# Attention: roots over four slots, projection and v chunks in other pairs, expert weights in pieces of 1024

## The chip, the cores and the metric

One core of a Trainium2 chip runs the whole program in one launch. The metric is device time in microseconds. The kernel before takes 1556.12 us as the median of three runs (1555.55 to 1556.91).

## The reference

x has 16 sequences of 256 rows and 256 columns. A first block (norms, a folded gate, a merge with a style vector, a feed-forward part) makes x1. Then comes attention, and then eight experts that each take the 512 rows with the highest gate. The change touches the attention stage, so this is the part that matters:

```python
h = _ln(x, ln1_g, ln1_b) + shift
qkv = (h @ Wqkv.T).reshape(b, n, 3, H, HD)          # H = 16 heads, HD = 64
q = _ln(qkv[:, :, 0].transpose(0, 2, 1, 3), qn_g, qn_b)
k = _ln(qkv[:, :, 1].transpose(0, 2, 1, 3), kn_g, kn_b)
v = qkv[:, :, 2].transpose(0, 2, 1, 3)
scores = jnp.einsum('bhnd,bhmd->bhnm', q, k) / jnp.sqrt(jnp.float32(HD))
attn = jax.nn.softmax(scores, axis=-1)
o = jnp.einsum('bhnm,bhmd->bhnd', attn, v)
x = x + o.transpose(0, 2, 1, 3).reshape(b, n, H * HD) @ Wout.T
gate = jax.nn.softmax(tok @ Wgate.T, axis=-1)        # tok: all 4096 rows of x
# each expert: g = _ln of its rows; gelu(g @ fc1s + b1s) @ fc2s + b2s, times the gate, added to the rows
```

Every large product is made of three fp32r matmuls: both operands are split into a high and a low part (h, l), and the product low times low is left out. The experts' weights fc1s and fc2s are split the same way, during the attention stage, and stored in DRAM for the expert stage.

## The kernel before

The attention stage works on one sequence (batch) per step t, t = -2 to 16. The steps 2 to 11 are a hardware loop of five passes with two steps each; the others are written out. Step t has eight pairs s, one for each two heads of batch t. While batch t has its scores made, batch t-1 is projected, batch t+1 has its q and k normed and its v made, batch t+2 is layer-normed and its first chunks made, and x2 of batch t-2 is finished. A pair has two slots, 2s and 2s+1. All engines run the same steps in their own order, which is written out by hand; a queue is strictly in order and semaphores join them.

In a pair TensorE does, in this order: the scores of pair s (L1019), the transposes of the probabilities of the pair before (L1032), the fill of slot 2s, the chunks of this pair, a half of the projection if slot 2s holds it, the values matmuls (L1045) of the pair before, the fill of slot 2s+1. A chunk is 6 matmuls of 512 columns of the qkv product (L147, `product`); chunks 0 to 7 are q and k, 8 to 11 are v. A half of the projection is 24 matmuls of 256 columns. A fill is a group of transposes into the one bank `tr`: of h (`a` of the next batch), of q and k (eight, "qk" 0 to 7, L1102), of x2, or the gate products; ScalarE empties the bank (`empty`) before the next fill may use it (`tr_free`). TR_FILLS says which fill stands in which slot, CHUNK_PAIRS which pair a chunk is in.

VectorE does in a pair: `lowest_of` (L1346, the row minima of both heads' scores, whose q side carries a minus sign, which ScalarE's exponentials wait for), the low half of the output (L1365), the reciprocal of side 0 (L1352), the copy of `pT` for side 1 (L1377), and in between the pieces of its chains. `chains` has, in each slot, six spots. A root chain (`rsqrt_op`, L93 to L100, and L1294 ahead of it) is 12 small dependent operations on 128x32 for n=0 and 12 for n=1. SUM_SLOT is the slot in which it starts, and in the kernel before one operation stands in every spot. `total` (L1342) sums the squares of a chunk. At the end of odd pairs stands the subtraction that makes `ew_l` (L1406). In pair 5 stands a_h (L1400), which waits for `out_h` and for all twelve chunks of batch t+1.

ScalarE does the low-lag work: o_h, emptying `tr`, four exponentials (L1158), the copy of `pT` for side 0 (L1221), the outputs of the chunks, and at the end of even pairs `ew_h` (L1232). GpSimd does the norms of q and k (`norm`, L1244, in slots NORM_SLOT to NORM_SLOT+3; the first of each n waits for the roots), the two divisions of the probabilities by their sums (`divide`, L1249), in pair 5 between both divisions a_l (L1274, waits for a_h), in pair 6 rstd (L1264) and the sum for x2 (L1268). SP issues the loads and stores. For the experts' weights it moves four pieces of 512 columns in each step: load `ew_raw`, wait for `ew_l`, store both parts, load the next.

Of the kernel before, what the change touches and what calls it, by code (L numbers as in the profile page):

```python
# [15 lines left out]
F32 = mybir.dt.float32  # L16
# [3 lines left out]
ALU = mybir.AluOpType  # L20
# [186 lines left out]
def first_block(nc, a, exponent, banks, ident, x1_rows, hbias, cols, target_rows, load_attention, weights, rows_of, sbuf, sems):  # L207
# [4 lines left out]
    with s:  # L212
# [179 lines left out]
        with nc.Block() as block:  # L392
# [414 lines left out]
TR_FILLS = [("x2", 0, 1), ("gates", 0, 3), ("proj", 0, 4), ("qk", 0, 5), ("qk", 1, 6), ("qk", 2, 7), ("h", 0, 8), ("qk", 3, 9),  # L807
            ("proj", 1, 10), ("qk", 4, 11), ("qk", 5, 12), ("qk", 6, 13), ("qk", 7, 14)]
# [6 lines left out]
CHUNK_PAIRS = [6, 6, 7, 7, 0, 0, 1, 1, 3, 3, 4, 4]  # L815
AHEAD = 4

SUM_SLOT, NORM_SLOT = (2, 6), (4, 8)
SPOTS = 6
LN_SLOT, ROOT_PAIR, APPLY_SLOT = 10, 6, 13  # L820
SPLIT_PAIR = 5
OUT_STATS_PAIR, OUT_ROOT_PAIR, OUT_APPLY_PAIR = 7, 1, 2
X2_PAIR = 6
# [43 lines left out]
def attention(nc, exponent, weights, rows_of, banks, ident, x1_rows, hbias, cols, x2_rows, logit, out, a, halves, sbuf, sems):  # L867
# [4 lines left out]
    with s:  # L872
# [21 lines left out]
        ew_raw = sbuf(s, "ew_raw", [P, 512])  # L894
        ew_h, ew_l = (sbuf(s, f"ew_{p}", [P, 512], F32R) for p in "hl")
# [61 lines left out]
        with nc.Block() as block:  # L957
            @block.sync
            def _(sp):
                def load_piece(b, c):  # L960
                    if c < 2:
                        src = a["fc1s"][bass.ds(b * P, P), c * 512:(c + 1) * 512]
                        dst = ew_raw[:, :]
                    else:
                        src = a["fc2s"][bass.ds(b * (4 * P) + (c - 2) * 2 * P, 2 * P), :].rearrange("(k p) n -> p k n", p=P)
                        dst = ew_raw[:, :].rearrange("p (k n) -> p k n", n=D)
                    sp.dma_start(dst, src).then_inc(ew_in, 16)

                def pieces(b, cs):
                    for c in cs:  # L970
                        if live(b):
                            wait(sp, ew_lo, 4, b, c + 1)
                            for n, part in enumerate((ew_h, ew_l)):
                                sp.dma_start(halves[c // 2 * 2 + n][bass.ds(b, 1), :, c % 2 * 512:(c % 2 + 1) * 512].rearrange("s p n -> p (s n)"),
                                             part[:, :].bitcast(F32)).then_inc(ew_stored, 16)
                        nb, nc_ = (b, c + 1) if c < 3 else (b + 1, 0)
                        if live(b) and live(nb):
                            load_piece(nb, nc_)
# [3 lines left out]
                def step(t, odd):  # L982
                    pieces(t, (0,))
# [10 lines left out]
                    pieces(t, (1,))  # L994
# [4 lines left out]
                    pieces(t, (2,))  # L999
# [4 lines left out]
                    pieces(t, (3,))  # L1004
# [3 lines left out]
                sp.wait_ge(ew_stored, 128 * NB)  # L1008
# [142 lines left out]
            def _(act):  # L1151
# [54 lines left out]
                def step(t, odd):  # L1206
                    for s in range(PAIRS):
# [21 lines left out]
                        if live(t) and s % 2 == 0:  # L1229
                            wait(act, ew_in, 64, t, 16 * (s // 2 + 1))  # L1230
                            wait(act, ew_stored, 128, t, 32 * (s // 2))
                            nc.scalar.activation(ew_h[:, :], ew_raw[:, :], ACT.Copy).then_inc(ew_hi, 1)  # L1232
# [48 lines left out]
            def _(dve):  # L1281
                link = Links(dve, links)

                def chains(t, i, spot):
# [3 lines left out]
                    for n in range(TT):  # L1288

                        k = (i - SUM_SLOT[n]) * SPOTS + spot  # L1290
                        if live(new) and 0 <= k <= RSQRT_OPS:
# [62 lines left out]
                def step(t, odd):  # L1354
                    far = t + 2
                    for s in range(PAIRS):
# [46 lines left out]
                        if live(t) and s % 2 == 1:  # L1403
                            wait(dve, ew_hi, 4, t, s // 2 + 1)
                            wait(dve, ew_stored, 128, t, 32 * (s // 2))
                            nc.vector.tensor_tensor(ew_l[:, :], ew_raw[:, :], ew_h[:, :].bitcast(F32), ALU.subtract).then_inc(ew_lo, 1)  # L1406
# [481 lines left out]
```

## Time and profile before

| | us |
|---|---|
| median of three runs | 1556.12 |
| the profiled execution, its own time | 1554.05 |
| its span, first to last instruction | 1551.9 |
| TensorE busy | 1380.8 (89%) |
| VectorE busy | 1019.5 (66%) |
| ScalarE busy | 959.8 (62%) |
| GpSimd busy | 783.3 (50%) |

The attention stage with scores runs from 398.7 us to about 1256 us of the span; in its middle TensorE is busy for 294.9 of 300 us. The granted clock of TensorE there is 1.00 of 2.4 GHz. In the timelines a row is one instruction, or several of the same kind in a row: start, length, engine, line, operation, tiles, shape and count; in brackets stands the idle time of the engine before it and what ended it. PE is TensorE, DVE VectorE, ACT ScalarE, POOL GpSimd. Matmuls overlap, so what counts is from start to start. Lines L93 to L147 are helpers.

### The profile page before, as it was taken

Reading aid. Unit: us, or ns where it says so; the run is one execution under the profiler, and the core shown is the slowest. Engines: PE = TensorE matmul, PEld = TensorE weight load, DVE = VectorE, ACT = ScalarE, POOL = GpSimd, SP = SyncE. Lnnn points to the kernel's source line nnn. Section 1 sums busy time; section 2 is a strip of 40 time slices with the busy share of each in tenths; the row PEclk is TensorE's granted clock in tenths of the full one; section 3 lists DMA queues with packets and bytes.
Section 4 is the critical chain, followed back from the end, with each engine's and each line's share of the span. In section 5 each row is a group of like instructions: output and inputs, shape, how many; then the busy total and the mean of one; then the engine's idle time right before and its main releaser. Section 6 shows DMA issues by size and latency. Waiting matters only on the chain. (4 is left out here: it accounts for less than half of the span.)

```text
span 1551.9 us, 31212 instructions
## 1 busy us (share of the span) xinstructions
PE 1380.8 (89%) x9672; PEld 1132.0 (73%) x9672; DVE 1019.5 (66%) x2495; ACT 959.8 (62%) x2535; POOL 783.3 (50%) x736
## 2 busy tenths in 40 slices
PE   1599999997899999999999999999999852599996
PEld 1599999996567777777777776777777642498996
DVE  2686666744566777776777777677767566565642
ACT  2266656564677777778777877877787620335452
POOL 1377666654346555645654654565455410254633
PEclk9799999999999999999999999999999975699998
DMA  7122222110022222212222221222222253167652
GB/s 233 44 64 63 68 74 61 50 47 28 21 69 82 82 82 77 82 61 76 88 82 71 86 82 62 75 88 82 76 75 82 83 184 128 39 205 234 203 161 27
DMA packets 92407, 138.89 MB, mean 89 GB/s; under 512 B 8656, under 2 KB 61824, under 8 KB 92160
## 3 DMA queue, kind: packets, MB, share of 16 engines
q1 hardware_dynamic: 83600, 126.02, 24.3%
q0 software_dynamic: 6144, 8.39, 2.9%
q10 hardware_dynamic: 2544, 3.16, 0.6%
q8 instruction: 42, 0.69, 0.2%
q14 instruction: 77, 0.63, 0.1%
HBM read 87.20 MB, written 50.35 MB: 89 GB/s over the span
## 5 line engine op out<-in xcount | busy, mean ns | idle before, releaser
L1249 POOL TENSOR_TENSOR prob<-prob,share_p 128x512 f32<-128x512 f32 x256 | 268.1, 1053 | 329.5 <-DVE share_p L1352 329.5
L1158 ACT ACTIVATE prob<-bank,shift 128x256 f32<-128x256 f32 x512 | 236.1, 474 | 110.0 <-DVE shift L1346 109.8
L1346 DVE TENSOR_REDUCE shift<-bank 128x2 f32<-128x512 f32 x256 | 164.7, 685 | 194.8 <-PE bank L1019 189.8
L1244 POOL TENSOR_TENSOR raw_qk<-raw_qk,rq 128x512 f32<-128x512 f32 x128 | 145.6, 1149 | 65.3 <-DVE rq L100 65.3
L147 PE MATMUL bank<-wqkv_h,rowsT_h 128*128 128x512 f32 x384 | 160.7, 418 | 4.4 <-PEq L392 3.5
L1045 PE MATMUL bank<-pT,v 128*64 128x256 f32 x1024 | 139.6, 394 | 25.3 <-ACT pT L1221 25.3
L147 PE MATMUL bank<-wqkv_h,rowsT_l 128*128 128x512 f32 x384 | 152.2, 396 | 0.0
L147 PE MATMUL bank<-wqkv_l,rowsT_h 128*128 128x512 f32 x384 | 151.7, 395 | 0.0
L1019 PE MATMUL bank<-landing 64*128 64x256 f32 x1024 | 146.3, 404 | 3.1 <-ACT prob L1158 3.1
L1032 PEld LDWEIGHTS bank<-ident,prob 128*128 128x128 f32 x1024 | 109.8, 141 | 44.5 <-issue 42.1
L1032 PE MATMUL bank<-ident,prob 128*128 128x128 f32 x1024 | 141.2, 280 | 0.6 <-POOL prob L1249 0.4
L1045 PEld LDWEIGHTS bank<-pT,v 128*64 128x64 f32 x1024 | 62.4, 136 | 82.3 <-issue 31.4
L1019 PEld LDWEIGHTS bank<-landing 64*128 64x128 f32 x1024 | 88.7, 187 | 34.4 <-issue 23.0
L1177 ACT ACTIVATE landing<-bank,cols 128x512 f32<-128x512 f32 x128 | 102.3, 799 | 11.6 <-PE bank L1102 11.6
L1158 ACT ACTIVATION_READ_ACCUMULATOR prob<-bank,shift 128x1 f32 x512 | 104.3, 204 | 0.0
L630 POOL TENSOR_TENSOR hid_l<-hid,hid_h 128x512 fp32r<-128x512 f32 x64 | 85.9, 1351 | 32.7 <-ACT hid_h L547 31.9
L1199 ACT ACTIVATE raw_sq<-bank 128x512 f32<-128x512 f32 x128 | 79.4, 620 | 30.2 <-DVE ssq L1342 30.2
L543 ACT ACTIVATE hid<-bank,cols 128x256 f32<-128x256 f32 x128 | 53.4, 471 | 69.6 <-PE bank L147 69.6
L1342 DVE TENSOR_REDUCE ssq<-raw_sq 128x8 f32<-128x512 f32 x128 | 86.1, 676 | 6.0 <-ACT raw_sq L1199 4.5
L1377 DVE COPY pT<-bank 128x512 f32<-128x512 f32 x128 | 88.1, 688 | 0.4 <-issue 0.3
L1102 PE MATMUL bank<-ident,raw_qk 128*128 128x128 f32 x512 | 82.4, 284 | 5.8 <-ACT landing L1177 4.4
L147 PEld LDWEIGHTS bank<-wqkv_h,rowsT_h 128*128 128x128 f32 x384 | 73.4, 191 | 18.4 <-issue 4.0
(286 smaller groups left out, 4044.3 us busy)
## 6 DMA issues: line engine op xcount, KB each, us to landing
ew_raw<-in_fc1s SPq DMA_DIRECT2D x32, 256.0 KB, 3.3
split_w1h<-ew_h SPq DMA_DIRECT2D x32, 256.0 KB, 2.0
split_w1l<-ew_l SPq DMA_DIRECT2D x32, 256.0 KB, 2.4
ew_raw<-in_fc2s SPq DMA_DIRECT2D x32, 256.0 KB, 3.0
split_w2h<-ew_h SPq DMA_DIRECT2D x32, 256.0 KB, 2.1
split_w2l<-ew_l SPq DMA_DIRECT2D x32, 256.0 KB, 2.5
ew_h<-split_w1h SPq DMA_DIRECT2D x8, 1024.0 KB
ew_l<-split_w1l SPq DMA_DIRECT2D x8, 1024.0 KB
```

The lines of the kernel that those rows point to most:

```text
L147: last = nc.tensor.matmul(out, a, b, start=(n == 0), stop=(n == 3 * len(ks) - 1))
L630: nc.gpsimd.tensor_tensor(hid_l[:, 2 * g:2 * g + 2, :], hid[:, 2 * g:2 * g + 2, :], hid_h[:, 2 * g:2 * g + 2, :].bitcast(F32), ALU.subtrac ...
L1019: mm = nc.tensor.matmul(score_bank[side][:, n * T:(n + 1) * T], qT[odd][r, s, n * P:(n + 1) * P], kT[odd][r, s, :], start=True, stop=True)
L1032: last = nc.tensor.transpose(pT_bank[side][:, m * T + n * P:m * T + (n + 1) * P], prob[q % 2 * 2 + side][:, n, m * P:(m + 1) * P], ident[: ...
L1045: last = nc.tensor.matmul(values_bank(b, q)[side * HD:(side + 1) * HD, 0:T], v[its][:, m, h * HD:(h + 1) * HD], pT[q % 2 * 2 + side][:, m, ...
L1158: last = nc.scalar.activation(prob[at][:, n, :], score_bank[side][:, n * T:(n + 1) * T], ACT.Exp, bias=shift[:, at, n:n + 1], scale=-1.0, ...
L1177: nc.scalar.activation(dst[its][:, j % 2 * 4:j % 2 * 4 + 4, j // 4 * P:(j // 4 + 1) * P], tr[:, :].rearrange("p (m n) -> p m n", m=4), ACT ...
L1244: nc.gpsimd.tensor_tensor(part, part, rq[:, n, c * 8:(c + 1) * 8].unsqueeze(2).to_broadcast([P, 8, HD]), ALU.mult).then_inc(normed, 1)
L1249: nc.gpsimd.tensor_tensor(prob[at][:, :, :], prob[at][:, :, :], share[:, at, :].unsqueeze(2).to_broadcast([P, TT, T]), ALU.mult).then_inc( ...
L1342: nc.vector.tensor_reduce(ssq[:, n, c * 8:(c + 1) * 8], raw_sq[c % 2][:, :].rearrange("p (h d) -> p h d", h=8), AX, ALU.add).then_inc(summ ...
L1346: nc.vector.tensor_reduce(shift[:, s % 2 * 2 + side, :], score_bank[side][:, :].rearrange("p (n m) -> p n m", n=TT), AX, ALU.min).then_inc ...
L1377: nc.vector.tensor_copy(pT[q % 2 * 2 + 1][:, :, :].rearrange("p m n -> p (m n)"), pT_bank[1][:, :]).then_inc(pT_dve, 1)
```

## The change

- TR_FILLS: h moves from slot 8 to 5, the second half of the projection from slot 10 to 6, and the eight q and k transposes from slots 5, 6, 7, 9, 11, 12, 13, 14 to the slots 7 to 14. The v chunks 8 to 11 move from pairs 3, 3, 4, 4 to pairs 4, 4, 5, 5.
- The root chains use the spots 0, 2 and 4 of a slot alone (ROOT_SPOTS): a chain takes four slots, 2 to 5 and 6 to 9, where it took two, 2 and 3 and 6 and 7. NORM_SLOT goes from (4, 8) to (6, 10).
- The experts' weights go in two pieces of 1024 columns a step instead of four of 512. `ew_h` is made in pairs 2 and 5 (before: 0, 2, 4, 6) and `ew_l` in pairs 3 and 6 (before: 1, 3, 5, 7). `ew_l` is now written in place over `ew_raw`, so the next load waits for both stores. SP's stores and loads stand at other places in its step.

```diff
-TR_FILLS = [("x2", 0, 1), ("gates", 0, 3), ("proj", 0, 4), ("qk", 0, 5), ("qk", 1, 6), ("qk", 2, 7), ("h", 0, 8), ("qk", 3, 9),
-            ("proj", 1, 10), ("qk", 4, 11), ("qk", 5, 12), ("qk", 6, 13), ("qk", 7, 14)]
+TR_FILLS = [("x2", 0, 1), ("gates", 0, 3), ("proj", 0, 4), ("h", 0, 5), ("proj", 1, 6)] + [("qk", j, 7 + j) for j in range(8)]
-CHUNK_PAIRS = [6, 6, 7, 7, 0, 0, 1, 1, 3, 3, 4, 4]
+CHUNK_PAIRS = [6, 6, 7, 7, 0, 0, 1, 1, 4, 4, 5, 5]
-SUM_SLOT, NORM_SLOT = (2, 6), (4, 8)
-SPOTS = 6
+SUM_SLOT, NORM_SLOT = (2, 6), (6, 10)
+SPOTS, ROOT_SPOTS = 6, (0, 2, 4)
+EW_HI_PAIRS, EW_LO_PAIRS = (2, 5), (3, 6)
-        ew_raw = sbuf(s, "ew_raw", [P, 512])
-        ew_h, ew_l = (sbuf(s, f"ew_{p}", [P, 512], F32R) for p in "hl")
+        ew_raw, ew_h = sbuf(s, "ew_raw", [P, DD]), sbuf(s, "ew_h", [P, DD], F32R)
+        ew_l = ew_raw[:, :].bitcast(F32R)
+                def store_piece(b, c):
+                    if live(b):
+                        wait(sp, ew_lo, 2, b, c + 1)
+                        for n, part in enumerate((ew_h[:, :], ew_l)):
+                            sp.dma_start(halves[2 * c + n][bass.ds(b, 1), :, :].rearrange("s p n -> p (s n)"), part.bitcast(F32)).then_inc(ew_stored, 16)
+
+                def next_piece(b, c):
+                    if live(b):
+                        wait(sp, ew_stored, 64, b, 32 * c)
+                        load_piece(b, c)
                 def step(t, odd):
-                    pieces(t, (0,))
...
-                    pieces(t, (1,))
+                    store_piece(t, 0)
                     b = t + 3
                     if live(b):
                         wait(sp, tr_h, 1, b - 1, 1)
                         sp.dma_start(x1[:, :, :], x1_rows[bass.ds(b * T, T), :].rearrange("(t p) d -> p t d", p=P)).then_inc(x1_in, 16)
-                    pieces(t, (2,))
+                    next_piece(t, 1)
...
-                    pieces(t, (3,))
+                    store_piece(t, 1)
+                    if not isinstance(t, int) or t >= 0:
+                        next_piece(t + 1, 0)
...
-                        if live(t) and s % 2 == 0:
-                            wait(act, ew_in, 64, t, 16 * (s // 2 + 1))
-                            wait(act, ew_stored, 128, t, 32 * (s // 2))
+                        if live(t) and s in EW_HI_PAIRS:
+                            c = EW_HI_PAIRS.index(s)
+                            wait(act, ew_in, 32, t, 16 * (c + 1))
+                            wait(act, ew_stored, 64, t, 32 * c)
                             nc.scalar.activation(ew_h[:, :], ew_raw[:, :], ACT.Copy).then_inc(ew_hi, 1)
...
-                        k = (i - SUM_SLOT[n]) * SPOTS + spot
-                        if live(new) and 0 <= k <= RSQRT_OPS:
+                        k = (i - SUM_SLOT[n]) * len(ROOT_SPOTS) + spot // 2
+                        if live(new) and spot in ROOT_SPOTS and 0 <= k <= RSQRT_OPS:
...
-                        if live(t) and s % 2 == 1:
-                            wait(dve, ew_hi, 4, t, s // 2 + 1)
-                            wait(dve, ew_stored, 128, t, 32 * (s // 2))
-                            nc.vector.tensor_tensor(ew_l[:, :], ew_raw[:, :], ew_h[:, :].bitcast(F32), ALU.subtract).then_inc(ew_lo, 1)
+                        if live(t) and s in EW_LO_PAIRS:
+                            c = EW_LO_PAIRS.index(s)
+                            wait(dve, ew_hi, 2, t, c + 1)
+                            nc.vector.tensor_tensor(ew_l, ew_raw[:, :], ew_h[:, :].bitcast(F32), ALU.subtract).then_inc(ew_lo, 1)
```

## Rows read from the trace of the kernel before

**Rows 1.** TensorE's waits, 500 to 1100 us: us in total, times, longest.
```profile
PE bank L1045 <- ACT pT L1221: 10.2, 15, 1.4
```

**Rows 2.** Busy time of two single pairs: stretch, its length, TensorE busy, clock.
```profile
682.18:689.17 6.99, 6.61 (x53) 1.00 0.40 128
649.09:655.62 6.53, 6.53 (x53) 1.00 0.00 1
```

**Rows 3.** Timeline of TensorE: `values` in both pairs.
```profile
654.02 1.08 PE L1045 MATMUL bank<-pT,v 128*64 128x256 f32 x8
...
687.57 1.08 PE L1045 MATMUL bank<-pT,v 128*64 128x256 f32 x8 [0.38 <-ACT pT L1221]
```

**Rows 4.** Timelines of VectorE and GpSimd around pairs 1 and 2.
```profile
656.79 1.29 DVE L1346 TENSOR_REDUCE shift<-bank 128x2 f32<-128x512 f32 x2 [1.82 <-PE bank L1019]
...
680.74 0.97 DVE L99 SCALAR_TENSOR_TENSOR rt<-rt,ssq 128x32 f32<-128x32 f32 x1
...
684.38 1.28 DVE L1346 TENSOR_REDUCE shift<-bank 128x2 f32<-128x512 f32 x2
...
680.63 1.04 POOL L1249 TENSOR_TENSOR prob<-prob,share_p 128x512 f32<-128x512 f32 x1 [1.09 <-DVE share_p L1352]
```

**Rows 5.** Timelines: the last chunk matmul of two pairs, and a consumer.
```profile
660.62 0.39 PE L147 MATMUL bank<-wqkv_h,rowsT_l 128*128 128x512 f32 x1
...
370.97 0.39 PE L147 MATMUL bank<-wqkv_h,rowsT_l 128*128 128x512 f32 x1
...
371.39 0.60 ACT L1197 ACTIVATE raw_qk<-bank 128x512 f32<-128x512 f32 x1 [0.29 <-PE bank L147]
```

**Rows 6.** Pair 2 of t=1 (timeline) and pairs 2 to 7 of t=0 (windows).
```profile
470.63 1.08 PE L1045 MATMUL bank<-pT,v 128*64 128x256 f32 x8 [1.34 <-ACT pT L1221]
...
409.05:418.82 9.77, 5.11 (x31) 0.85 0.22 82
418.82:452.51 33.69, 31.13 (x201) 0.99 0.16 56
```

**Rows 7.** Timelines of VectorE and GpSimd in pair 3.
```profile
694.13 0.98 DVE L99 SCALAR_TENSOR_TENSOR rt<-rt,ssq 128x32 f32<-128x32 f32 x1
695.14 0.97 DVE L100 SCALAR_TENSOR_TENSOR rq<-rt,rq 128x32 f32<-128x32 f32 x1
...
694.02 1.04 POOL L1249 TENSOR_TENSOR prob<-prob,share_p 128x512 f32<-128x512 f32 x1 [0.62 <-DVE share_p L1352]
695.02 1.05 POOL L1244 TENSOR_TENSOR raw_qk<-raw_qk,rq 128x512 f32<-128x512 f32 x1
```

**Rows 8.** Two lines over the whole run: ns min/median/max, first and last.
```profile
L1406 DVE TENSOR_TENSOR ew_l<-ew_raw,ew_h x64: 673/686/1170, 412.1 to 1250.6; 128x512 fp32r<-128x512 f32 x64
...
L1274 POOL TENSOR_TENSOR rowsT_l<-rowsT,rowsT_h x15: 1266/1567/1654, 387.1 to 1143.0; 128x512 fp32r<-128x512 f32 x15
```

**Rows 9.** Timelines of VectorE, GpSimd and TensorE in pairs 5 and 6.
```profile
653.94 0.43 DVE L1400 CAST rowsT_h<-rowsT 128x512 fp32r<-128x512 f32 x1
...
654.53 1.56 POOL L1274 TENSOR_TENSOR rowsT_l<-rowsT,rowsT_h 128x512 fp32r<-128x512 f32 x1 [1.21 <-DVE rowsT_h L1400]
656.05 1.05 POOL L1249 TENSOR_TENSOR prob<-prob,share_p 128x512 f32<-128x512 f32 x1
657.05 1.05 POOL L1244 TENSOR_TENSOR raw_qk<-raw_qk,rq 128x512 f32<-128x512 f32 x1
658.05 0.69 POOL L1264 TENSOR_TENSOR rstd<-var_eps,exponent 128x2 f32<-128x2 f32 x1
658.70 1.30 POOL L1268 TENSOR_TENSOR x<-proj,x 128x512 f32<-128x512 f32 x1
...
657.64 0.60 PE L1102 MATMUL bank<-ident,raw_qk 128*128 128x128 f32 x4
```

**Rows 10.** DMA issues of the page: count, KB each, us to landing.
```profile
ew_raw<-in_fc1s SPq DMA_DIRECT2D x32, 256.0 KB, 3.3
```

**Rows 11.** Timeline of TensorE in step t=-1: the first q and k transpose.
```profile
375.61 0.66 PE L1102 MATMUL bank<-ident,raw_qk 128*128 128x128 f32 x4 [1.40 <-POOL raw_qk L1244]
```

More of the change, by code:

```diff
@@ L960, in load_piece @@
                 def load_piece(b, c):
-                    if c < 2:
-                        src = a["fc1s"][bass.ds(b * P, P), c * 512:(c + 1) * 512]
-                        dst = ew_raw[:, :]
-                    else:
[L965 to L978, printed above, removed]
+                    if c == 0:
+                        sp.dma_start(ew_raw[:, :], a["fc1s"][bass.ds(b * P, P), :]).then_inc(ew_in, 16)
+                    else:
+                        sp.dma_start(ew_raw[:, :].rearrange("p (k n) -> p k n", n=D),
+                                     a["fc2s"][bass.ds(b * (4 * P), 4 * P), :].rearrange("(k p) n -> p k n", p=P)).then_inc(ew_in, 16)
+                def store_piece(b, c):
[7 more added lines that the diff above has]
+                        load_piece(b, c)
                 load_piece(0, 0)
                 def step(t, odd):
-                    pieces(t, (0,))
                     b = t - 2
@@ L1007, in _ @@
                 sp.wait_ge(x2n_stored, 16 * NB)
-                sp.wait_ge(ew_stored, 128 * NB)
+                sp.wait_ge(ew_stored, 64 * NB)
             @block.tensor
```

## The prediction

> **What bounds the kernel now.** I read the waits of TensorE first, then the length of single pairs, then each engine's timeline around the pairs that are too long. In the middle of the attention stage TensorE sits idle for 10.2 us in 600, in 15 places, always in front of the matmuls of `values`, for ScalarE's copy of `pT` [rows 1]. So the stage is TensorE's queue, and only what removes such a wait, or makes a new one, can move the time. A batch is a step t of eight pairs s, and I count within a pair from its first score matmul (+0). A pair with half a projection takes 6.53 us where nothing is late (649.09), but 6.99 us in pair 2 (682.18) [rows 2]: there `values` starts at +5.39 instead of +4.93 [rows 3].
>
> Why it is late: VectorE starts `lowest_of` at +2.20 instead of +1.17, because the root chain of tiles n=0 (twelve small operations in slots 2 and 3, that is in pair 1) runs over into pair 2. One of them, L99 at 680.74, lasts 0.97 us instead of 0.19: it ends 0.04 us after the division that GpSimd began at 680.63 [rows 4]. From `lowest_of` to `values` it takes 687.57-684.38 = 3.19 us [rows 3, 4]. So `values` can start at (start of `lowest_of`)+3.19, normally at +4.36, and a pair bears this much lateness without loss: 0.57 us with a projection (`values` is due at +4.93), 0.95 us with a qk transpose and two chunks (due at +5.3, 0.3 after the last chunk matmul at 660.62 [rows 5]).
>
> The longest of the 15 waits is 1.4 us [rows 1]: that kind stands in pair 0 of every other batch, where the loop's body begins anew, and the change doesn't touch it. Four of these at 1.3 and eleven of pair 2 at 0.45 make up the 10.2 us.
>
> **The parts, step by step.** The numbers of matmuls, activations and small operations stay as they are, but for the weights (below).
>
> *Roots over four slots.* Pair 1 now holds six operations. Before its end only the fourth meets a division, and VectorE is free at about +6.8, while `lowest_of` of pair 2 is due at 6.88+1.17. In pair 2 the other six, two x2n operations and two sums end at about +7.5, with `lowest_of` of pair 3 due at 6.53+1.17 = 7.70. The stall of pair 2 goes: 13 batches (t=2 to 14; 0.46 here, more in some) x 0.5 = **-6.5**; t=1 lost 1.34 there [rows 6], **-0.9** on top; the same lateness in pair 4 of t=14 **-0.3**.
>
> *What is late next: pair 3.* Its six operations are followed by the subtraction for `ew_l`, now 1024 wide. GpSimd's second division started at +4.85 (694.02); now two root operations stand ahead of its reciprocal instead of three, so about +4.65. Behind it come norm(7) and, since the norms of n=0 now fill slots 6 to 9, norm(8) without a gap: ends at 5.7, 6.7 and 7.7, with a pitch of 1.0 us. VectorE's L99 and L100 each got through only as one GpSimd operation ended (0.98 and 0.97 us) [rows 7]. The last two roots of pair 3 then end at 6.7 and 7.7. Whether L97 is held as well (0.19 us unheld; 0.98 if like L99) changes nothing here: one of the GpSimd operations is waited out anyway. The subtraction costs 0.69 us for 512 columns [rows 8]; its pitch to the next operation is 0.6, for 1024 about 1.14 (0.07 fixed, the rest doubled). `lowest_of` of pair 4 starts at 8.85 instead of 7.70, 1.15 late against a margin of 0.95: **+0.2** a batch (0 if the last root slips in ahead of norm(8), 0.5 if another operation is held), 14 x 0.2 = **+2.8**. For t=0, where pair 3 has no projection and is 0.6 shorter, +0.8.
>
> *v chunks in pairs 4 and 5.* VectorE's a_h (L1400) and GpSimd's a_l (L1274) in pair 5 wait for all 12 chunks. The last two were in pair 4; now they are in pair 5 itself, in front of that wait. The last chunk matmul of a pair starts at +5.00 (660.62), and a consumer starts 0.42 after such a matmul (370.97 to 371.39) [rows 5]: a_h at +5.4 instead of 653.94-649.09 = +4.85. Nothing else is queued behind it on VectorE until `lowest_of`. On GpSimd division 1 and norm(11) are. a_l begins 0.16 after a_h's end, so at about +5.95; it lasts 1.56 where `ew_l` runs beside it, 1.27 at the shortest [rows 8, 9], and `ew_l` leaves pair 5, so I take 1.27. Division 1 ends at +8.2; it was 8.0. It is due at TensorE at 6.88+1.57 = 8.45: no wait. norm(11) ends at +9.2. Before, it ended at 658.10, at pair 6's +2.5, and slot 14 in pair 7 took it, so nobody waited; now slot 12 in pair 6 takes it, at 6.88+2.0 = 8.9 (657.64 is such a fill, 2.02 into its pair) [rows 9]. TensorE waits to 9.33: **+0.45** a batch. With a_l at 1.56 it is 0.75, with everything 0.1 us quicker 0.35. t=0 to 13: **+6.3**.
>
> *GpSimd in pair 6.* It gets norm(12) and norm(13) beside rstd, the x2 sum and two divisions (rstd 0.65, the sum 1.3, the others 1.0 each [rows 7, 9]). Counted now from pair 6's start, norm(11) ends at +2.3, so norm(13) at +8.3; the 1.1 us subtraction and two `x1` operations of VectorE fall in between, and if the subtraction holds GpSimd for its length it is +9.3. The fill of slot 14 is due at 6.88+0.45+2.0 = +9.3. Margin 0 to 1 us; cost taken **+0.5** in all.
>
> *h transposes in slot 5, projection in 2 and 3.* ScalarE empties h before pair 3's exponentials, at about +1.3, and the projection there needs the bank at +1.9. Nothing, and up to 0.1 a batch if `ew_h` (1024 wide, about 1.1 us) is late.
>
> *Weights by 1024.* 64 activations, 64 subtractions and 192 DMA issues become half as many. Their work lies on ScalarE, VectorE and SP beside TensorE's. SP stores in pairs 3 and 6, the activations are in pairs 2 and 5; the tighter of the two loads is issued late in pair 4, once both stores have landed, and needed at about +6 of pair 5, some 8 us later, where 256 KB took 3.3 us [rows 10]. On SP the x1 load stands behind the store of pair 3 and ahead of its use in pair 5; the output store waits behind a load of pair 4 and was due in pair 6. No cost. In t=0, `ew_h` no longer stands ahead of pair 1's exponentials: **-0.4**.
>
> *Start.* In t=0 pair 2 loses most: TensorE is busy for 5.11 of 9.77 us [rows 6], because twelve roots and `ew_l` stand ahead of `lowest_of`, and then qk 0 waits for its norm. Now h stands in that slot and qk 0 a pair later. Pairs 2 to 7 of t=0 took 9.77+33.69 = 43.5 us [rows 6], and take 6.2+6.0+4 full pairs (27.0) = 39.2 without the new stalls: **-4.3**, and +0.8 for pair 4 (its +0.45 is counted). In t=-1, where nothing covers, the roots of n=0 now stand behind two more sums, so qk 0 goes from 375.61 [rows 11] to about 377.9; qk 5 stands behind chunk 11, a_h, a_l and norm(11): **+2.2**, with 1 to 5 as ends, since TensorE idles longer before the chunks and its clock may fall.
>
> Sum: -6.5-0.9-0.3-0.4-4.3 = -12.4 against 2.8+0.8+6.3+0.5+2.2 = +12.6, so +0.2 us on the profiled 1554.05 (span 1551.9), and so **1556.3 us** on the median of 1556.12 (the profiled execution is 2 us under it).
>
> **A rule of the Trainium skill.** In "SBUF — State Buffer", section "Who interferes with whom", VectorE operations with two SBUF inputs, and copies or tensor_scalar in a two-port mode, share one pair of ports with GpSimd, and whichever begins first holds it for its whole length. The rows agree: 0.97 and 0.98 for an operation of 0.19 [rows 4, 7]. By it L97 is held too, and the 1024-wide subtraction would hold GpSimd for its length; the sum stays, but it speaks against the wider piece, and so for the third rival.
>
> **Rivals.** (1) *The forecast*: the wait of pair 2 moves to pairs 4 and 6. Own range 1553 to 1559. Chance 0.42.
> (2) *Faster: one of the two new stalls is not there.* If the last root of pair 3 gets in ahead of norm(8), 2.8+0.8 go: 1552.7. If a_l is through sooner, 14 x 0.3 more go: 1548.5. For it: both margins are a few tenths. Against: the chunks stand ahead of a_h by program order, and two operations in a row were held [rows 7]. Chance 0.26.
> (3) *Slower: GpSimd's run from a_l to norm(13) is too long for pairs 5 and 6.* It has nine operations in the 10.2 us from +5.95 of pair 5 to slot 14's fill. If a_l takes 1.56 (+0.3 x 14 = 4.2), or the subtraction and the `x1` operations hold it for over 1 us in pair 6, slot 14 waits as well. Each 0.1 us behind +9.3 costs 1.3 us; 0.3 us is 4. Together 1561 to 1564. For it: a_l took 0.3 us more where a subtraction of 512 overlapped it [rows 8, 9]. Against: the x1 operations slowed GpSimd by under 0.1. Chance 0.27.
> (4) *The roots aren't what makes pair 2 late* (ScalarE or the bank is): -6.5-0.9 do not come, 1563.7. Against it: `lowest_of` is late by 1.03 us in just the pair after the chain. Chance 0.05.
>
> **Range and chances.** Within 0.2% (3.1 us) is about what a measurement of this kernel can tell from no change. Rival 2 reaches from 1548.5, rival 3 to 1564; I take 1549.5 to 1563. Faster by over 0.2% 0.28 (rival 2 with the low end of the forecast), within 0.43, slower 0.29 (rivals 3 and 4).
>
> **What would show it.** In the changed profile, `lowest_of` of pair 2 at +1.17 and no wait of `values` there; in pair 4 a wait of 0.2 us for ScalarE's `pT`; in pair 6 a wait of TensorE's qk transposes (L1102 of before) for GpSimd's norm, with a_h at +5.4 in pair 5; pair 2 of t=0 at about 6.2 us. Wrong would be a_h at its old place, or a wait for `shared` or for h's bank in pair 3.

## The result and the profile after

The kernel after takes 1557.54 us (median of 12 runs, 1556.33 to 1559.18), the kernel before 1554.57 us in the same comparison: a ratio of 1.0018, 95% interval 1.0009 to 1.0026. That is 3.0 us more by the medians (2.8 by the ratio), where +0.2 was forecast. The time itself is 1.2 us above the forecast of 1556.3 and inside its range of 1549.5 to 1563.0. It comes that near because the forecast set out from 1556.12, a median of three runs, and over twelve runs the kernel before takes 1.6 us less. By the bound set ahead (0.2%) it is no change, but the whole interval lies on the slower side of 1 and its upper end is over that bound.

The profiled executions lie somewhat further apart: 1558.74 us (span 1556.7) after, 1554.05 (span 1551.9) before, a difference of 4.7 us (the one is 1.2 us above the median of its kernel, the other 0.5 us below). All sums below are of these two executions.

TensorE's waits between 500 and 1100 us, after (us in total, times, longest):

```profile
PE bank L1044 <- ACT pT L1220: 6.7, 4, 1.7
PE bank L1101 <- POOL raw_qk L1244: 2.9, 11, 0.3
```

The same view of the kernel before is [rows 1]. (Lines of TensorE and ScalarE are one number lower in the kernel after, so L1044 is `values`, L1101 the qk transposes, L1406 the subtraction for `ew_l` as before.) The eleven waits of pair 2 are gone: four are left, those at the loop's head, and they have grown from at most 1.4 to 1.7 us. In their place stands one wait a batch for GpSimd's norm, eleven in all. The wait of 0.2 us in pair 4 for `pT`, which the forecast named as a sign, is not in this list: there `values` only starts at +5.42 where +5.28 is its time without a wait. `lowest_of` of pair 2 (begun at 685.31) comes at +1.17, as forecast:

```profile
686.48 1.29 DVE L1346 TENSOR_REDUCE shift<-bank 128x2 f32<-128x512 f32 x2 [1.41 <-PE bank L1018]
```

Now the eight pairs of one batch (t=5) after, TensorE's busy time in each; and three of the same batch before, which [rows 2] does not have:

```profile
671.96:678.44 6.48, 6.48 (x43) 1.00 0.19 75
678.44:685.31 6.87, 6.87 (x45) 1.00 0.00 1
685.31:691.85 6.54, 6.54 (x54) 1.00 0.10 34
691.85:698.39 6.54, 6.54 (x54) 1.00 0.16 46
698.39:705.41 7.02, 6.96 (x45) 1.00 0.52 188
705.41:712.30 6.89, 6.89 (x45) 1.00 0.25 76
712.30:719.67 7.37, 7.10 (x45) 1.00 0.10 37
719.67:726.06 6.39, 6.39 (x41) 1.00 0.45 172
```
```profile
696.06:702.94 6.88, 6.88 (x45) 1.00 0.45 152
709.48:716.39 6.91, 6.91 (x45) 1.00 0.44 152
716.39:722.69 6.30, 6.30 (x42) 1.00 0.00 0
```

Columns: stretch, its length, TensorE busy with the count of matmuls, granted clock, DMA share, GB/s. The second fence is pairs 4, 6 and 7. Pair 2 fell from 6.99 [rows 2] to 6.54; pairs 3 and 5 have exchanged their work (6.89 and 6.54 became 6.54 and 6.89); pair 4 rose by 0.14, pair 6 by 0.46, pair 7 by 0.09. A batch is 0.24 us longer: the wait was moved, not removed.

Pairs 3 to 6 of the same batch after, on VectorE and GpSimd (start, us, engine, line):

```profile
696.58 0.98 DVE L97 TENSOR_TENSOR rt<-rq 128x32 f32<-128x32 f32 x1
697.60 0.97 DVE L99 SCALAR_TENSOR_TENSOR rt<-rt,ssq 128x32 f32<-128x32 f32 x1
698.60 0.97 DVE L100 SCALAR_TENSOR_TENSOR rq<-rt,rq 128x32 f32<-128x32 f32 x1
699.49 1.21 DVE L1406 TENSOR_TENSOR ew_raw<-ew_raw,ew_h 128x1024 fp32r<-128x1024 f32 x1
700.63 1.27 DVE L1346 TENSOR_REDUCE shift<-bank 128x2 f32<-128x512 f32 x2
...
710.81 0.43 DVE L1400 CAST rowsT_h<-rowsT 128x512 fp32r<-128x512 f32 x1 [0.47 <-PE bank L147]
```
```profile
696.48 1.04 POOL L1249 TENSOR_TENSOR prob<-prob,share_p 128x512 f32<-128x512 f32 x1 [0.40 <-DVE share_p L1352]
697.48 2.04 POOL L1244 TENSOR_TENSOR raw_qk<-raw_qk,rq 128x512 f32<-128x512 f32 x2
...
711.40 1.27 POOL L1274 TENSOR_TENSOR rowsT_l<-rowsT,rowsT_h 128x512 fp32r<-128x512 f32 x1 [1.76 <-DVE rowsT_h L1400]
712.63 1.04 POOL L1249 TENSOR_TENSOR prob<-prob,share_p 128x512 f32<-128x512 f32 x1
713.63 2.04 POOL L1244 TENSOR_TENSOR raw_qk<-raw_qk,rq 128x512 f32<-128x512 f32 x2
```

Three operations that last 0.19 us by themselves (L97, L99, L100) each wait out one GpSimd operation: division 1, norm(7), norm(8). The subtraction stands behind them, and `lowest_of` of pair 4 starts at 700.63-698.39 = +2.24 (forecast +2.31), against a limit of +2.11. In pair 5 a_h starts at 710.81-705.41 = +5.40, exactly as forecast, a_l at +5.99 with 1.27 us, and norm(11), the first of the two in the last row, ends about 714.7. The fill of slot 12 in TensorE's timeline shows the wait:

```profile
714.73 0.66 PE L1101 MATMUL bank<-ident,raw_qk 128*128 128x128 f32 x4 [0.27 <-POOL raw_qk L1244]
```

It starts at +2.43 of pair 6 instead of +2.0.

Where the 4.7 us come from, by the starts of the first score matmuls in both traces:

| stretch | forecast, us | profiled, us |
|---|---|---|
| up to the first scores of t=0 (398.73 to 403.14) | +2.2 | +4.4 |
| t=0 | -3.4 | -1.7 |
| t=1 | -0.3 | -0.6 |
| t=2 to 13 without the loop's heads | +2.3 | +2.3 |
| four heads of the loop's body (pair 0) | 0 | +1.6 |
| t=14 and t=15 | -0.6 | -1.2 |
| sum | +0.2 | +4.8 |

The forecast's column is its own terms put to the batches they were worked out for (in the fourth row twelve times -0.5+0.2+0.45, and the 0.5 for slot 14).

### The profile page after: what moved, and what is told of

The parts are those of the page before. It is cut to its first block and busy times, and to the rows that moved or that the text cites. A ratio compares the mean times of both kernels' runs of the same rounds, so it can differ in the third digit from the quotient of the medians.

```text
span 1556.7 us, 30827 instructions
## 1 busy us (share of the span) xinstructions
PE 1386.4 (89%) x9672; PEld 1133.7 (73%) x9672; DVE 1075.9 (69%) x2463; ACT 956.7 (61%) x2503; POOL 778.3 (50%) x736
## 5 line engine op out<-in xcount | busy, mean ns | idle before, releaser
L1044 PE MATMUL bank<-pT,v 128*64 128x256 f32 x1024 | 139.5, 394 | 18.2 <-ACT pT L1220 17.2
L1044 PEld LDWEIGHTS bank<-pT,v 128*64 128x64 f32 x1024 | 62.3, 136 | 75.0 <-issue 33.3
L1101 PE MATMUL bank<-ident,raw_qk 128*128 128x128 f32 x512 | 82.7, 285 | 12.8 <-POOL raw_qk L1244 10.3
L1101 PEld LDWEIGHTS bank<-ident,raw_qk 128*128 128x128 f32 x512 | 56.1, 142 | 42.3 <-issue 25.6
```

Of the source, the lines that this page charges most:

```text
L1044: last = nc.tensor.matmul(values_bank(b, q)[side * HD:(side + 1) * HD, 0:T], v[its][:, m, h * HD:(h + 1) * HD], pT[q % 2 * 2 + side][:, m, ...
L1101: last = nc.tensor.transpose(tr[:, m * P:(m + 1) * P], raw[:, j, m * P:(m + 1) * P], ident[:, :])
```

## The experiments

Eight kernels, each compared with the kernel before (1555.31 us for e1 to e4, 1555.28 for the others) and to be read against the kernel after, 1557.54. That one was measured on another occasion, on which the kernel before took 1554.57, so a difference of under 1 us from it says nothing. Pair lengths are those of t=5 in each profile; "heads" are the pairs 0 of t=4, 6, 8 and 10, which stand behind the loop's branch; "first scores" is where t=0 begins in the span:

| kernel | us | pair 2 | pair 3 | pair 4 | pair 5 | pair 6 | pair 7 | heads, mean | first scores |
|---|---|---|---|---|---|---|---|---|---|
| before | 1555.3 | 6.99 | 6.89 | 6.88 | 6.54 | 6.92 | 6.29 | 7.82 | 398.7 |
| after | 1557.5 | 6.54 | 6.54 | 7.02 | 6.89 | 7.37 | 6.39 | 8.22 | 403.1 |
| e1_al_last | 1546.5 | 6.54 | 6.54 | 7.03 | 6.89 | 6.88 | 6.29 | 8.07 | 400.3 |
| e2_load_after_head | 1554.8 | 6.54 | 6.54 | 7.02 | 6.89 | 7.37 | 6.39 | 7.85 | 402.6 |
| e3_roots_n0_two_slots | 1560.4 | 6.54 | 6.54 | 7.03 | 6.90 | 7.38 | 6.40 | 8.34 | 400.1 |
| e4_weights_512 | 1558.4 | 6.54 | 6.54 | 6.90 | 6.88 | 7.67 | 6.29 | 7.80 | 401.7 |
| e5_dense_roots_start | 1557.8 | 6.54 | 6.54 | 7.03 | 6.90 | 7.38 | 6.40 | 8.69 | 400.2 |
| e6_weights_alone | 1556.1 | 6.54 | 6.90 | 7.36 | 6.57 | 6.89 | 6.29 | 8.11 | 399.8 |
| c1_three_edits | 1544.6 | 6.54 | 6.54 | 7.03 | 6.90 | 6.88 | 6.29 | 7.81 | 397.8 |
| c2_norm8_behind_div | 1539.8 | 6.54 | 6.53 | 6.90 | 6.88 | 6.88 | 6.29 | 7.80 | 397.9 |

**The wait of pair 6: a_l behind what does not need it.** Theory: pair 6 waits only because norm(11) is queued behind a_l. Rival: it is a_h and a_l themselves that come too late for TensorE.

```diff
                         if live(t):
                             divide(t, s, 0)
+                        if live(t):
+                            divide(t, s, 1)
+                        norm(new, 2 * s + 1)
                         if live(far) and not first(far) and s == SPLIT_PAIR:
                             wait(pool, a_hi, 1, far, 1)
                             wait(pool, chunk_done, 12, far - 1, 12)
                             nc.gpsimd.tensor_tensor(a_l[:, :, :], aT[:, :, :], ...)
-                        if live(t):
-                            divide(t, s, 1)
-                        norm(new, 2 * s + 1)
```

> The kernel after with one edit: in pair 5 GpSimd does division 1 and norm(11) first and a_l behind them (before: a_l in front of both). Theory: pair 6 is 0.45 us too long only because a_h (at +5.40) holds up what stands behind a_l on GpSimd. With the edit norm(11) ends near +6.7 of pair 5, slot 12 in pair 6 finds it done; a_l ends near +1.0 of pair 6 and chunk 0 needs it at +2.4. norm(13) moves forward with the rest of the run, to about +8.0 of pair 6 against a fill due at +8.9. So pair 6 goes from 7.37 to 6.92 and pair 7 from 6.39 to 6.29, 13 times 0.55 = 7.2 us; in t=-1 the wait of 2.50 us before qk 5 shrinks to about 1.0, 1.5 us more. Together about 9 us under the kernel after, 1548.5 beside 1554.6 for the kernel before. Rival: it is the late a_h and a_l themselves that TensorE meets; then chunk 0 in pair 6 waits in place of the fill, or slot 14 in pair 7 does, and the time stays within 2 us of the kernel after.

Measured: 1546.5 us (1546.02 to 1547.57), ratio to before 0.9944 (0.9930 to 0.9957), 11.0 us under the kernel after. Pairs 6 and 7 are 6.88 and 6.29, and the batch 53.53 instead of 54.10. GpSimd in pairs 5 and 6, and the fill of slot 12:

```profile
704.72 1.04 POOL L1249 TENSOR_TENSOR prob<-prob,share_p 128x512 f32<-128x512 f32 x1 [0.42 <-DVE share_p L1352]
705.72 1.30 POOL L1244 TENSOR_TENSOR raw_qk<-raw_qk,rq 128x512 f32<-128x512 f32 x1
706.98 1.26 POOL L1277 TENSOR_TENSOR rowsT_l<-rowsT,rowsT_h 128x512 fp32r<-128x512 f32 x1
708.21 1.04 POOL L1244 TENSOR_TENSOR raw_qk<-raw_qk,rq 128x512 f32<-128x512 f32 x1
```
```profile
708.96 0.60 PE L1101 MATMUL bank<-ident,raw_qk 128*128 128x128 f32 x4
```

norm(11) ends at 707.0, with pair 6 begun at 706.97; the fill comes at +1.99 with no wait, and a_l, done at 708.2 (+1.3), is in time for chunk 0. The rival falls. The gain is 2 us over the expected 9. A batch gives 0.57 where 0.55 was expected; the start gives 2.8 us instead of 1.5, where the second wait of t=-1 for GpSimd (2.50 us, below) became one of 1.01 for ScalarE; the heads give 0.6; and pair 7 of t=14 gives 0.9, which ran at a granted clock of 0.74 in the profiled execution of after.

**The head of the loop.** The body's first pair took 7.82 us in the mean before and 8.22 after, which the forecast did not have. Theory: the 512 KB load of the next batch's weights now runs while VectorE and ScalarE fetch the instructions at the branch. Rival: VectorE's stream is another one there, with no subtraction at its end.

```diff
                 def step(t, odd):
+                    if (not isinstance(t, int) or t > 0) and live(t):
+                        wait(sp, ew_stored, 64, t, 0)
+                        wait(sp, exped, H, t, 2)
+                        load_piece(t, 0)
 ...
                     store_piece(t, 1)
-                    if not isinstance(t, int) or t >= 0:
-                        next_piece(t + 1, 0)
```

> The kernel after with one edit: SyncE loads the first weight piece of batch t once pair 0 of t has its exponentials, not at the end of pair 7 of t-1. Theory: pair 0 at the loop's head became 8.2 instead of 7.8 us because the 512 KB load runs just while VectorE and ScalarE fetch the loop's first instructions (lowest_of at +3.33 instead of +2.58). With the edit lowest_of comes back to about +2.6 and the four pairs to about 7.8: 4 times 0.43 = 1.7 us under the kernel after, nothing else moves. Rival: the later start at the head comes from the instructions themselves (VectorE's stream at the end of the body is another one, with no subtraction behind the last total); then the four pairs stay at 8.2 and the time stays.

Measured: 1554.81 us (1553.68 to 1555.61), ratio 0.9996 (0.9987 to 1.0005), 2.7 us under the kernel after. The heads are 7.88, 7.96, 7.93 and 7.64 instead of 8.29, 8.19, 8.19 and 8.20. VectorE's timeline at the head of t=4, after (pair begun at 616.04) and with the load moved (614.71):

```profile
615.97 0.67 DVE L1342 TENSOR_REDUCE ssq<-raw_sq 128x8 f32<-128x512 f32 x1
619.37 1.29 DVE L1346 TENSOR_REDUCE shift<-bank 128x2 f32<-128x512 f32 x2 [2.73 <-issue]
```
```profile
617.08 1.29 DVE L1348 TENSOR_REDUCE shift<-bank 128x2 f32<-128x512 f32 x2 [1.77 <-issue]
```

The DMA queues (packets, MB, share of the 16 engines) in the same pair, after: the first 1.3 us, then the next 0.9; and with the load moved the first 1.3 us:

```profile
q1 hardware_dynamic: 105, 0.42, 91.2%
...
q14 instruction: 2, 0.02, 5.0%
```
```profile
q14 instruction: 1, 0.01, 2.5%
```

After, the data queue takes 91.2% of the DMA engines' time in these 1.3 us, and not one instruction packet is among them; two come in the next 0.9 us, when the load is through. With the load moved, one instruction packet comes in that stretch, and VectorE's gap at the branch falls from 2.73 to 1.77 us. Nothing in VectorE's stream was changed, so the rival falls. All four heads say the same. The first instruction packet starts at +1.32 to +1.38 in the kernel after and at +0.25 to +0.32 with the load moved, and `lowest_of` starts 1.9 to 2.1 us behind it in both.

The heads are worth 1.5 us. The profiled executions lie 3.9 us apart; the rest of that is ahead of the first scores (0.6), in t=0 (0.8) and in t=14 (1.0). In t=0 both ran a part of a pair at a lower clock, in t=14 only that of after.

**What made pair 2 late.** Theory: the roots' overrun, as forecast. Rival: something else that was moved. The roots of n=0 go back to two slots:

```diff
+                        dense = n == 0
-                        k = (i - SUM_SLOT[n]) * len(ROOT_SPOTS) + spot // 2
-                        if live(new) and spot in ROOT_SPOTS and 0 <= k <= RSQRT_OPS:
+                        k = (i - SUM_SLOT[n]) * SPOTS + spot if dense else (i - SUM_SLOT[n]) * len(ROOT_SPOTS) + spot // 2
+                        if live(new) and (dense or spot in ROOT_SPOTS) and 0 <= k <= RSQRT_OPS:
```

> The kernel after with one edit: the roots of tiles n=0 again in two slots (2 and 3, that is in pair 1), those of n=1 stay spread over four. Theory: the chain runs over into pair 2 as before, lowest_of there starts about 1 us late (+2.2), pair 2 goes from 6.54 to 7.0, pair 3 stays at 6.54 or under: 13 times 0.45 = about 6 us over the kernel after; in t=-1 the first norm comes 2.2 us sooner, which takes 2.2 off, so +4 in all. Rival: pair 2 was late for the projection's place or for x2n, not for the roots; then pair 2 stays at 6.54 and the time falls by 2.

Measured: 1560.36 us (1558.05 to 1562.26), ratio 1.0039 (1.0026 to 1.0053). The time rose by 2.8 us, but not in the place expected: **pair 2 stays at 6.54 in every batch from t=2 on.** Only t=0 (8.00) and t=1 (7.34), whose pair 1 is 1 us shorter, have a late pair 2. VectorE there in t=5, pair 2 begun at 685.50:

```profile
684.06 0.97 DVE L99 SCALAR_TENSOR_TENSOR rt<-rt,ssq 128x32 f32<-128x32 f32 x1
...
686.89 0.19 DVE L100 SCALAR_TENSOR_TENSOR rq<-rt,rq 128x32 f32<-128x32 f32 x1
687.00 1.28 DVE L1347 TENSOR_REDUCE shift<-bank 128x2 f32<-128x512 f32 x2
```

The held L99 and the overrun into pair 2 are as in the kernel before [rows 4], yet `lowest_of` starts at +1.50, not +2.20. What is missing is the subtraction for `ew_l`, which stood between the last root and `lowest_of` in the kernel before and has gone to pair 3. So the lateness of 1.03 us was 0.33 of roots and 0.70 of subtraction, and 0.33 alone is under the margin of 0.57. The 2.8 us of the medians are not placed. The profiled execution, 1558.05 us, was the fastest of five and even 0.7 us under that of the kernel after: t=0 and t=1 gave +2.2 and +0.8, the heads +0.5, the start -3.1 and t=14 -1.1.

**The same from the other side: the weights part alone on the kernel before.**

```diff
-CHUNK_PAIRS = [6, 6, 7, 7, 0, 0, 1, 1, 4, 4, 5, 5]
+CHUNK_PAIRS = [6, 6, 7, 7, 0, 0, 1, 1, 3, 3, 4, 4]
-SUM_SLOT, NORM_SLOT = (2, 6), (6, 10)
+SUM_SLOT, NORM_SLOT = (2, 6), (4, 8)
+                        dense = True
```

(TR_FILLS is that of before as well; the diff is against the kernel after.)

> The kernel before with the weights part alone: two pieces of 1024 columns, activations in pairs 2 and 5, subtractions in pairs 3 and 6; roots, fills and chunks as before. Theory (formed from the run with the roots of n=0 in two slots): pair 2 was late by 1.03 us, of which 0.69 was the subtraction at the end of pair 1 and only 0.33 the roots' overrun, and 0.33 is inside the margin of 0.57. So pair 2 falls from 7.0 to 6.54 with the roots untouched, 13 times: 6 us less. In pair 4 lowest_of came at +2.02 already; with 0.53 us more of subtraction it comes at +2.55 and values waits about 0.45 us, 14 times: 6 us more. Loop heads as in the kernel after (7.8 to 8.2): 1 to 2 us more. Sum 0 to +2 us against the kernel before. Rival (the forecast's reading): the roots alone make pair 2 late, so that it stays at 7.0, and the time rises by 7 or more.

Measured: 1556.11 us (1553.21 to 1558.46), ratio 1.0009 (1.0000 to 1.0018). Pair 2 is 6.54 with the roots untouched, and pair 4 is 7.36 in t=5 (7.25 in the first batch of each loop body). The last root, subtraction and `lowest_of` of pair 4 (begun at 696.17), and its `values`:

```profile
697.49 0.19 DVE L100 SCALAR_TENSOR_TENSOR rq<-rt,rq 128x32 f32<-128x32 f32 x1
697.60 1.22 DVE L1408 TENSOR_TENSOR ew_raw<-ew_raw,ew_h 128x1024 fp32r<-128x1024 f32 x1
698.74 1.28 DVE L1348 TENSOR_REDUCE shift<-bank 128x2 f32<-128x512 f32 x2
```
```profile
701.93 1.08 PE L1045 MATMUL bank<-pT,v 128*64 128x256 f32 x8 [0.42 <-ACT pT L1221]
```

`lowest_of` at +2.57, `values` 3.19 behind it: the arithmetic of the forecast again. With both terms as expected the rival, that the roots alone make pair 2 late, is out.

**The weights part alone undone.** The pieces of 512 columns from the kernel before are put back (buffers, loads, stores, an activation in each even pair and a subtraction in each odd one); the rest is the kernel after:

```diff
-                        if live(t) and s in EW_LO_PAIRS:
-                            c = EW_LO_PAIRS.index(s)
-                            wait(dve, ew_hi, 2, t, c + 1)
+                        if live(t) and s % 2 == 1:
+                            wait(dve, ew_hi, 4, t, s // 2 + 1)
+                            wait(dve, ew_stored, 128, t, 32 * (s // 2))
```

> The kernel after with the weights part alone undone: four pieces of 512 columns, activations in pairs 0, 2, 4, 6, subtractions in pairs 1, 3, 5, 7. Theory: the subtraction of pair 3 takes 0.6 us less, so pair 4 loses its 0.14 us (14 times: 2 us), the four loop heads go back to 7.8 (1.7 us) and pair 7 to 6.29 (1.3 us); but in pair 5 the subtraction now stands behind a_h and beside a_l, a_l takes 1.56 instead of 1.27 us, and the fill of slot 12 waits 0.3 us more, 14 times: 4 us. Sum about 1 us under the kernel after. Rival: the wider piece as such costs or saves nothing on TensorE's path; then pairs 4, 6 and 7 keep their lengths.

Measured: 1558.37 us (1554.55 to 1558.91), ratio 1.0016 (1.0007 to 1.0025), 0.8 us over the kernel after where 1 under was expected; by the ratios (1.0016 and 1.0018) the two are equal. Pair by pair every term came: pair 4 7.02 to 6.90, pair 7 6.39 to 6.29, the heads to 7.80, and pair 6 from 7.37 to 7.67. In the profile they make -1.1 us, as expected (heads -1.7, t=2 to 13 without them +0.6). But that execution, 1554.55 us, was the fastest of eleven; the other 3.1 us by which it is under that of the kernel after lie mainly in the start, t=0 and t=14, and the median shows none of them. Why is open. GpSimd's a_l beside the subtraction (t=4):

```profile
653.92 0.69 DVE L1406 TENSOR_TENSOR ew_l<-ew_raw,ew_h 128x512 fp32r<-128x512 f32 x1
654.17 1.56 POOL L1274 TENSOR_TENSOR rowsT_l<-rowsT,rowsT_h 128x512 fp32r<-128x512 f32 x1 [1.75 <-DVE rowsT_h L1400]
```

1.56 us as in [rows 9], 1.27 without the neighbour, and TensorE pays the 0.3. In pair 4 (t=4, begun at 641.30) the last root is held as before, yet `lowest_of` comes at +1.70, inside the limit of +2.11, for the subtraction between them is 0.68 us long:

```profile
641.51 0.97 DVE L100 SCALAR_TENSOR_TENSOR rq<-rt,rq 128x32 f32<-128x32 f32 x1
643.00 1.28 DVE L1346 TENSOR_REDUCE shift<-bank 128x2 f32<-128x512 f32 x2
```

Pair 2 is 6.54 here too, this time with a subtraction in pair 1 and the roots spread. So the wait of pair 2 is gone with either of two parts of the change, the spread roots or the weights.

**The start.** The roots take every spot of two slots in the two steps before t=0:

```diff
+                        dense = isinstance(t, int) and t < 0
```

(and the two lines that use it, as above)

> The kernel after with one edit: in the two steps before the first batch (t=-2 and t=-1), where no scores run, the roots again take every spot of two slots. Theory: the first qk transpose of t=-1 waited 3.13 us for its norm; it comes at about 375.6 instead of 377.8, and the chunk behind it may keep the high clock (1.5 us more). The first scores of t=0 come 2 to 4 us sooner than 403.1, the pairs after that stay: 1554 to 1556 beside 1557.5 for the kernel after. Rival: the second half of t=-1 (a_h behind chunk 11, then qk 5 waits 2.5 us for norm(11)) is what sets the first scores; then they stay at 403.

Measured: 1557.79 us (1553.20 to 1558.88), ratio 1.0015 (1.0007 to 1.0024), that is no gain in the median. In the profiled execution (1555.84 us) the first scores come at 400.2 instead of 403.1 and the first wait for the norm is gone, as the theory says; but one head took 9.87 us, at a clock of 0.85. Its twelve runs are 5.7 us apart, so that a gain of 2 us can neither be shown nor excluded by it alone. Open.

**Together.** c1 is the order of e1, the load of e2 and the start of e5.

> Three edits on the kernel after at once: a_l behind division 1 and norm(11), the weight load behind pair 0, dense roots before the first batch. Theory: they touch different places and add up: a_l alone gave 1546.5; the load takes 1 to 1.5 us off the loop heads (8.07 in the mean there), the dense start 2 us: about 1543. Rival: with the start's norms sooner, TensorE meets a_l or the x1 rows there and the start gives nothing; then 1545.

Measured: 1544.63 us (1542.86 to 1545.46), ratio 0.9933 (0.9921 to 0.9946). It is 1.9 us under e1 where 3.5 was expected. In the profiles both terms are there: the first scores come at 397.8, 2.5 us sooner, and the heads are 7.81 in the mean, together 1.1 less. But these two executions were the slowest of e1's five and the fastest of c1's, so how much of it holds is open.

c2 adds one edit for pair 4, in GpSimd's step:

```diff
-                        norm(new, 2 * s)
+                        if s != 4:
+                            norm(new, 2 * s)
 ...
                         if live(t):
                             divide(t, s, 0)
+                        if s == 4:
+                            norm(new, 2 * s)
```

> The same three edits and a fourth: in pair 4 GpSimd does division 0 first and norm(8) behind it. Theory: pair 4 is 0.14 us too long because the last root of pair 3 (L100, begun at +0.21 of pair 4) waits out norm(8) until +1.18 and the subtraction and lowest_of (+2.24, margin to +2.11) stand behind it. With norm(8) gone from there L100 takes 0.19, the subtraction ends near +1.5, lowest_of starts by +1.5 and pair 4 falls from 7.03 to 6.88: 14 times 0.15 = 2 us under the kernel with three edits. Rival: the subtraction itself is what is too long, or the division waits now; then pair 4 stays at 7.0 or pair 5 grows.

Measured: **1539.77 us** (1539.32 to 1539.86), ratio 0.9902 (0.9888 to 0.9917), 15.5 us under the kernel before. Pair 4 (from 688.30):

```profile
687.52 0.97 DVE L99 SCALAR_TENSOR_TENSOR rt<-rt,ssq 128x32 f32<-128x32 f32 x1
688.52 0.19 DVE L100 SCALAR_TENSOR_TENSOR rq<-rt,rq 128x32 f32<-128x32 f32 x1
688.63 1.22 DVE L1412 TENSOR_TENSOR ew_raw<-ew_raw,ew_h 128x1024 fp32r<-128x1024 f32 x1
689.77 1.28 DVE L1352 TENSOR_REDUCE shift<-bank 128x2 f32<-128x512 f32 x2
```

With norm(8) out of the way L100 takes 0.19 us, the subtraction is still 1.22, `lowest_of` starts at +1.47 and pair 4 falls to 6.90. So pair 4 repeats pair 2: the hold of the root (0.78 us) and the wider subtraction (0.54 more than with 512) stand in front of `lowest_of`, together they pass the margin, and either gone is enough, the first here, the second in e4. TensorE's waits from 500 to 1100 us are then one line, the loop's heads:

```profile
PE bank L1046 <- ACT pT L1222: 5.0, 4, 1.4
```

The median fell by 4.9 us where 2 was expected; the profile gives 3.2 of it (first to last scores 836.2 and 833.0 us), of which t=0 has 0.8. c1's profiled execution was its fastest, and c2 ran four times; the rest is open.

## Why the prediction was right, and where it was not

**The stall of pair 2 goes: right in size, wrong in its cause.** It was put wholly on the roots at -6.5 us; t=2 to 13 gave 6.3 in their pairs 2. (Of the 1.34 us in t=1 only 0.9 was counted, though t=1 is not among the thirteen batches. With all of it the forecast for t=1 is -0.7, and -0.6 was profiled.) The forecast had the pieces for more: a lateness of 1.03 us, a margin of 0.57 and a subtraction with a pitch of 0.6 standing in that very pair. It never asked which of them alone would be enough. Both e4 (roots spread, subtraction there: `lowest_of` at +1.17) and e3 and e6 (roots dense, subtraction gone: +1.50) have 6.54. The part "roots over four slots" was thus not needed for the 6.5 us once the weights part was in: e3, with the roots of n=0 back in two slots, has the same pair lengths from t=2 on. What the spreading of the n=1 roots does by itself no run shows. The fourth rival, the roots are not the cause, was held at 0.05; what holds is in between, that the wait had two causes, either of which could go.

**Pair 4: right, 0.14 for 0.2.** +2.24 for +2.31, and the pitch of the wide subtraction, put at 1.14 with a fixed 0.07 in it that no row shows, is 1.14 (699.49 to 700.63). That L97 is held as well (0.98 us at 696.58), which was left open, made no difference, as said.

**Pair 6: right, 0.46 for 0.45.** a_h at +5.40, a_l 1.27, the fill at +2.43 for +2.45. e1 shows that the cause is the order on GpSimd.

**Pair 7: 0.09 for 0.04 a batch.** norm(13) starts at 719.63 and takes 2.02 us, ending 1.98 into pair 7:

```profile
718.69 2.06 DVE L1406 TENSOR_TENSOR ew_raw<-ew_raw,ew_h 128x1024 fp32r<-128x1024 f32 x1
...
719.63 2.02 POOL L1244 TENSOR_TENSOR raw_qk<-raw_qk,rq 128x512 f32<-128x512 f32 x1
```

This is the case the forecast counted with: the subtraction begins within a division, waits it out, and GpSimd's norm then waits for the subtraction. The rule of the Trainium skill in "SBUF — State Buffer", "Who interferes with whom" (one port pair, held for a whole instruction by whoever begins first), gives this row too.

**The start: a term that was mis-sized.** The first wait is 3.13 us and qk 0 comes at 377.76, 2.15 late, against a forecast of 2.2. What makes 4.4 of it is the clock. Behind that wait TensorE runs the next two chunks at the lower of its two clock levels (1.2 GHz) for most of their length: a matmul lasts 0.63 us where it had been 0.39, and the two chunks take 4.38 us (window 380.57 to 384.95, granted clock 0.62), where they took 2.84 before at a clock of 1.00 (from 377.61). At their end TensorE is 4.50 late. The fill of slot 12 then waits 2.50 us for norm(11), which stands behind chunk 11, a_h and a_l:

```profile
377.76 1.12 PE L1101 MATMUL bank<-ident,raw_qk 128*128 128x128 f32 x4 [3.13 <-POOL raw_qk L1244]
...
381.14 0.63 PE L147 MATMUL bank<-wqkv_l,rowsT_h 128*128 128x512 f32 x1
...
392.89 0.65 PE L1101 MATMUL bank<-ident,raw_qk 128*128 128x128 f32 x4 [2.50 <-POOL raw_qk L1244]
```

This wait adds nothing to the 4.4: the kernel before had one fill more in the same place, with waits of its own, and the chunks behind it start 4.07 late. But it kept TensorE from catching up, as e1 shows (first scores 2.8 us sooner). The forecast named both the clock and this chain and gave 1 to 5; 4.4 is inside, but the value taken counted the first wait only.

**t=0: -1.7 for -3.4.** Pair 2 took 7.21 us instead of 6.2 in the profiled execution, at a granted clock of 0.81; in that of e2, with the same work there, it took 5.96 at 1.00:

```profile
413.51:420.72 7.21, 5.01 (x31) 2.95 (x29) 5.95 (x17) 4.60 (x14) 2.79 (x4) 0.81 0.01 3
```
```profile
412.96:418.91 5.95, 3.75 (x30) 2.44 (x28) 5.31 (x15) 4.59 (x14) 2.11 (x3) 1.00 0.01 4
```

But in e2 the lower clock came a pair later (pair 3: 7.07 us at 0.83), and t=0 is still 0.9 us short of the forecast. Only e5 has both pairs at 5.96 and 1.00, and its t=0 takes 50.5 us, 3.3 less than before. So the step is right for the work; the clock, which the forecast left out here, takes 1 us or more of it in most executions profiled. Pair 4 of t=0 rose by 0.8, as forecast.

**The loop's heads: not forecast at all, +1.6.** Of the wait where the loop's body begins anew the forecast said "the change doesn't touch it", and of the weights' loads "No cost". It looked at who waits for the loaded data. It did not look at what else uses the DMA engines in the 3.5 us of a load, which now runs from 1.2 us before the head to 2.3 us into it; before, it was issued at +2.5.

**The total: near in part by luck.** Two missing terms (+2.2 at the start, +1.6 at the heads) and t=0's clock (+1.7) were in one direction, t=1 and the last two batches gave 0.9 back, and so 4.8 us came for 0.2. The medians are only 3.0 apart, and the forecast set out from a time that was 1.6 too high; both made the miss look smaller. What was right by its reasoning is that two new stalls eat what the old one gives.

What makes executions of one kernel lie up to 5.7 us apart (e5, twelve runs; c2 has 0.5, of four) the runs don't settle. The stretches at the lower clock in t=-1, in t=0 and in one loop head all come behind waits of TensorE, but which wait brings one is not shown: the same wait of 2.20 us leaves pair 2 of t=0 at 0.81 in after and at 1.00 in e2, and in t=-1 of the kernel before a stretch at 0.67 came behind waits of 1.0 us.

## What to carry to other kernels

When something is late, list everything that stands in front of it in its queue and subtract each item alone from the lateness before you compare it with the margin: two changes that each suffice are worth one, and the second adds only what it costs. On an engine that works in order, put an operation whose input comes late behind those that don't need it; here that one swap was worth 11 us, after a change that as a whole had cost 3. And a bulk transfer that nobody waits for still has to stay off the moment at which a loop branches.

## What the runs showed of the hardware

At the loop's branch VectorE sat idle in "issue" (it waits for nothing else that the profile shows) for 2.73 us with a 512 KB load in flight, and for 1.77 and 1.61 with the load moved (e2, c2). Before the change it was 1.28 with a subtraction of 0.68 us in front; from the end of the last `total` it is 1.88. The instruction packets come late when the data queue has 91% of the DMA engines' time. In e1, where the load ran until about +1.4, two heads took 7.9 us and two 8.2: the first instruction packet starts at +0.82 and +0.84 in the former, at +1.37 and +1.39 in the latter. The Trainium skill, in "Runtime: NRT & Kernel Launch", "Instruction fetch mechanics", says that a taken branch to a target outside the current window forces a fetch by DMA before execution can go on. The gaps agree with that; the wait behind data is what these runs add.

A two-input VectorE operation of 128x1024 takes 1.21 us at the shortest and 2.06 when it meets a GpSimd operation, and the GpSimd operation behind it then takes 2.02 instead of 1.04.
